# Transposing the first tile of y with a DMA and reordering VectorE's last stage-one work

## What is computed

```python
def fake_quant(x, scale, zp):
    q = clip(round(x / scale + zp), 0, 255)
    return (q - zp) * scale

def lora_ffn(x, W_up, gate_w, expert_bias, lora_A, lora_B):
    logits = x @ gate_w.T + expert_bias            # 4 experts
    one_hot = jax.nn.one_hot(argmax(logits), 4)
    base = x @ W_up.T
    z = einsum('nh,erh->ner', x, lora_A)           # rank 8
    delta = einsum('neh,ne->nh', einsum('ner,ehr->neh', z, lora_B), one_hot)
    return base + delta

x = x + tanh(g_xattn) * (fake_quant(layernorm(x)) @ fake_quant(ctx))
x = x + tanh(g_ffn) * lora_ffn(layernorm(x))
```

## Time and profile before

| | us |
|---|---|
| median of 3 runs | 956.85 (956.59 to 957.64) |
| the profiled execution, its own time | 955.6 |
| span of the profile | 953.8 |
| TensorE busy in matmuls | 933.3 |
| VectorE busy | 472.6 |
| ScalarE busy | 231.3 |
| GpSimd busy | 16.6 |

### The profile page before, as it was taken

How to read it: one execution, slowest core, us unless ns; L and a number is a source line. 1 busy time by engine, 2 the same in 40 slices (tenths; PEclk the granted TensorE clock), 3 DMA queues, 4 the chain that set the end, 5 groups by cost and what they waited for, 6 DMA issues and landing times.

```text
span 953.8 us, 12333 instructions
## 1 busy us (share of the span) xinstructions
PE 933.3 (98%) x5190; PEld 498.3 (52%) x5214; DVE 472.6 (50%) x1022; ACT 231.3 (24%) x192; POOL 16.6 (2%) x40
## 2 busy tenths in 40 slices
PE   4999999999999999999999999999999999999998
PEld 2444444444555555555555555555555555555554
DVE  7774757787775725244351625344342615343322
ACT  6976777776540100000000000000000000000000
POOL 0000100000000000000000000000000000000000
PEclk9999999999999999999999999999999999999999
DMA  8999977679564422222223222222223222121211
GB/s 347 421 416 415 397 291 276 223 299 316 222 181 133 133 89 45 89 45 89 56 78 95 75 96 45 89 45 89 45 89 89 68 66 45 45 45 45 45 45 45
DMA packets 85370, 137.37 MB, mean 144 GB/s; under 512 B 70224, under 2 KB 70368, under 8 KB 71008
## 3 DMA queue, kind: packets, MB, share of 16 engines
q1 hardware_dynamic: 79376, 94.83, 31.2%
q0 software_dynamic: 3488, 24.92, 6.7%
q10 hardware_dynamic: 2448, 16.78, 4.3%
HBM read 90.38 MB, written 29.37 MB: 126 GB/s over the span
## 4 chain that ended last, share of the span: by engine, by line
PE 96%; ACT 2%; DVE 1%; DMA 1%; issue 0%; SPq 0%; ACTq 0%; DVEq 0%
PE bank L1131 71%; PE bank L1049 22%; PE bank L1140 1%; PE bank L1026 1%; DMA rows<-in_x 1%; ACT arena L446 1%; ACT halves L416 0%; ACT rows_T L434 0%; DVE bn L638 0%; PE bank L1123 0%; DVE arena L709 0%; SPq L294 0%; PE bank L1146 0%; DVE rows L826 0%; DVE ln L642 0%
## 5 line engine op out<-in xcount | busy, mean ns | idle before, releaser
L1131 PE MATMUL bank<-arena,rows_T 128*128 128x416 f16 (+1 forms) x3840 | 683.0, 339 | 0.0
L1131 PEld LDWEIGHTS bank<-arena,rows_T 128*128 128x128 f16 x3840 | 372.5, 97 | 304.5
L1049 PE MATMUL bank<-arena,rows_T 128*128 128x512 bf16 x1000 | 222.0, 380 | 2.7 <-DVE arena L709 1.5
L1049 PEld LDWEIGHTS bank<-arena,rows_T 128*128 128x128 bf16 x1024 | 99.5, 98 | 119.8 <-issue 2.9
L826 DVE SCALAR_TENSOR_TENSOR rows<-bank,derived,rows 128x416 f32<-128x416 f32 (+2 forms) x80 | 49.7, 640 | 210.6 <-PE bank L1131 210.6
L485 ACT ACTIVATE z_stack_T<-bank 96x128 f16<-96x128 f16 x16 | 4.4, 273 | 555.3 <-PE bank L1146 555.3
L638 DVE BATCH_NORM_STATS2 bn<-rows 128x6 f32<-128x512 f32 x124 | 76.7, 678 | 4.2 <-DMA rows<-in_x 3.7
L766 DVE SCALAR_TENSOR_TENSOR route<-bank,derived,scal 128x4 f32<-128x4 f32 x16 | 3.5, 221 | 110.2 <-PE bank L1131 110.2
L699 DVE SCALAR_TENSOR_TENSOR rows<-bank,derived,rows 128x512 f32<-128x512 f32 x60 | 44.8, 747 | 25.7 <-PE bank L1049 25.2
L834 DVE SCALAR_TENSOR_TENSOR rows<-bank,z_back_scale,rows 128x512 f32<-128x512 f32 x64 | 45.1, 746 | 9.6 <-PE bank L1140 5.6
L739 DVE SCALAR_TENSOR_TENSOR halves<-normed,ln,halves 128x2048 f16<-128x2048 f32 x14 | 32.9, 2351 | 29.0 <-ACT halves L479 29.0
(11 more groups left out here) (107 smaller groups left out, 287.8 us busy)
## 6 DMA issues: line engine op xcount, KB each, us to landing
arena<-in_ctx SPq DMA_DIRECT2D x22, 1024.0 KB, 16.8
stage<-in_w SPq DMA_DIRECT2D x17, 1042.0 KB, 6.2
out<-rows ACTq DMA_DIRECT2D x15, 1024.0 KB, 3.9
h_scratch<-rows POOLq DMA_DIRECT2D x11, 1024.0 KB, 8.7
rows<-h_scratch SPq DMA_DIRECT2D x11, 1024.0 KB, 4.8
stage<-in_ctx SPq DMA_DIRECT2D x10, 1024.0 KB, 9.1
rows<-in_x POOLq DMA_DIRECT2D x10, 1024.0 KB, 9.0
normed<-in_w SPq DMA_DIRECT2D x7, 1042.0 KB, 6.8
```

The source lines that it names most:

```text
L1049: mm = mmul(bk, q1T[:, t % 4, kt, :], Q(b, n, kt), start=(kt == 0), stop=(kt == KT - 1 and not slow), skip_group_check=True)
L1131: mm = mmul(bank[c][:, 0:b - a], YT[:, s % 2, yh, kt, :], W(kt, wh, a, b), start=(first and kt == kts[0] and yh == 0 and wh == 0), stop=(k ...
```

## The change

Tile 0 of y is transposed by DMA as well. SyncE issues `y_transpose(0)` between W's loads 15 and 16, and the 32 TensorE transposes are gone. `yT_out` becomes `yT_scale`, which scales `YT` in place in SBUF for both tiles and, for tile 0, waits for the DMA transpose. On VectorE `epi(15, 1)` and `epi(15, 2)` now stand ahead of `w_low(8)`, and the second to fourth scalings of tile 0 come later, between and behind `w_low(9)` to `w_low(11)`. The counts of the semaphore `s_dt` go up by one transfer wherever it is waited for.

```diff
@@ -35,7 +35,6 @@
     LEAD = 3
     KEEP = 4
 
-    BY_PE = 1
     UNSCALED = 2
     HALF = KT // 2
 
@@ -170,8 +169,6 @@
 
         bank = [es.enter_context(nc.psum_tensor(f"bank{i}", [P, NB], F32)) for i in range(8)]
         TR = [bank[5][:, :], bank[6][:, :]]
-
-        YB = [TR[0], TR[1], bank[7][:, :], TR[0]]
         ZP = bank[7][:, :].bitcast(F16)[0:ZR, 0:P]
 
         s_scal = sem("scal_loaded"); s_braw = sem("b_loaded"); s_bs = sem("b_abs_sum"); s_bp = sem("b_pow")
@@ -195,7 +192,7 @@
         s_sum = sem("w_abs_sum"); s_wp = sem("w_pow"); s_wa = sem("w_scale"); s_hi = sem("w_high")
         s_lo = sem("w_ready")
         s_pm = sem("pow_max"); s_PM = sem("pow_max_all")
-        s_yh = sem("y_high"); s_yl = sem("y_low"); s_yt = sem("yT_group"); s_ye = sem("yT_out")
+        s_yh = sem("y_high"); s_yl = sem("y_low"); s_ye = sem("yT_scaled")
         s_wc = sem("w_back_scale"); s_wr0 = sem("w_back_row_parked"); s_wr = sem("w_back_row_loaded")
         s_xt = {t: sem(f"q1_transposed_by_dma{t}") for t in BY_DMA}; s_dt = sem("y_transposed_by_dma")
         s_m2 = sem("chunk2_done"); s_dl = sem("delta_done"); s_rt = sem("route_step"); s_zs = sem("z_stack_ready"); s_gl = sem("z_back_scale_ready")
@@ -312,6 +309,15 @@
             row(5)
             for c in range(16, CT):
                 ctx_tile(c)
+            def y_transpose(s):
+                sp.wait_ge(s_yl, s + 1)
+                if s < UNSCALED:
+                    sp.wait_ge(s_mm, place[(13 if s == 0 else 15, NCH - 1)] + 1)
+                else:
+                    sp.wait_ge(s_m2, 5 * (s - 1))
+                sp.dma_start_transpose(YT[:, s % 2].rearrange("p h k m -> p (h k) m"),
+                                       HL[:, :, :].rearrange("p h d -> p (h d)")).then_inc(s_dt, 16)
+
             def q1_transpose(t):
                 sp.wait_ge(s_q1, t + 1)
                 sp.wait_ge(s_mm, place[(t - 4, NCH - 1)] + 1)
@@ -323,24 +329,18 @@
             for i in range(12, 14):
                 load_w(i)
             q1_transpose(15)
-            for i in range(14, KT + 8):
+            for i in range(14, KT):
                 load_w(i)
-
-            def y_transpose(s):
-                sp.wait_ge(s_yl, s + 1)
-                if s == 1:
-                    sp.wait_ge(s_mm, place[(TILES - 1, NCH - 1)] + 1)
-                else:
-                    sp.wait_ge(s_m2, 5 * (s - 1))
-                sp.dma_start_transpose(YT[:, s % 2].rearrange("p h k m -> p (h k) m"),
-                                       HL[:, :, :].rearrange("p h d -> p (h d)")).then_inc(s_dt, 16)
+            y_transpose(0)
+            for i in range(KT, KT + 8):
+                load_w(i)
 
             sp.wait_ge(s_wc, 1)
             sp.dma_start(wrow_d.rearrange("k p -> p k"), wc[:, :],
                          allow_slow_non_contiguous=True).then_inc(s_wr0, 16)
             sp.wait_ge(s_wr0, 16)
             y_transpose(1)
-            sp.wait_ge(s_dt, 16)
+            sp.wait_ge(s_dt, 32)
             sp.dma_start(WR, wrow_d.rearrange("k p -> (k p)").unsqueeze(0).to_broadcast([P, D])).then_inc(s_wr, 16)
             for s in range(UNSCALED, TILES):
                 if s + 3 < TILES:
@@ -398,7 +398,7 @@
             nc.gpsimd.dma_start(br[:, :], brow_d.rearrange("k o -> (k o)").unsqueeze(0).to_broadcast(
                 [P, E * R])).then_inc(s_br, 16)
             pool.wait_ge(s_bst, 1)
-            pool.wait_ge(s_dt, 16)
+            pool.wait_ge(s_dt, 32)
             row(TILES + KEEP)
 
         @block.scalar
@@ -467,11 +467,8 @@
                 act.wait_ge(s_norm, s + 1)
                 if s == 0:
                     transposed(act, TILES - 1)
-                elif s <= BY_PE:
-                    act.wait_ge(s_yt, 4 * s)
-                    act.wait_ge(s_yl, s)
                 else:
-                    act.wait_ge(s_dt, 16 * (s - BY_PE))
+                    act.wait_ge(s_dt, 16 * s)
                 u = TILES + s
                 if s < UNSCALED:
                     A(HL[:, 0, :], Xt(u), ACT.Identity, bias=L(u, "nmr"), scale=L(u, "rstd")).then_inc(s_yh, 1)
@@ -732,24 +729,16 @@
             def y_low(s):
                 dve.wait_ge(s_yh, s + 1)
                 if s < UNSCALED:
-                    if s >= 1:
-                        dve.wait_ge(s_yt, 4 * s)
                     v.tensor_tensor(HL[:, 1, :], T[:, 0:D], HL[:, 0, :], ALU.subtract).then_inc(s_yl, 1)
                 else:
                     v.scalar_tensor_tensor(out=HL[:, 1, :], in0=T[:, 0:D], scalar=L(TILES + s, "rstd"), in1=HL[:, 0, :],
                                            op0=ALU.mult, op1=ALU.subtract).then_inc(s_yl, 1)
 
-            def yT_out(s, g):
-                dst = YT[:, s % 2, :, 4 * g:4 * g + 4, :]
-                if s < BY_PE:
-                    dve.wait_ge(s_yt, 4 * s + g + 1)
-                    dve.wait_ge(s_mm, place[(13, NCH - 1)] + 1)
-                    src = YB[g].bitcast(F16).rearrange("p (h a m) -> p h a m", h=2, a=4)
-                else:
-                    dve.wait_ge(s_dt, 16)
-                    src = dst
+            def yT_scale(s, g):
+                dve.wait_ge(s_dt, 16 * (s + 1))
+                part = YT[:, s % 2, :, 4 * g:4 * g + 4, :]
                 back = wc[:, 4 * g:4 * g + 4].unsqueeze(1).unsqueeze(3).to_broadcast([P, 2, 4, P])
-                v.tensor_tensor(dst, src, back, ALU.mult).then_inc(s_ye, 1)
+                v.tensor_tensor(part, part, back, ALU.mult).then_inc(s_ye, 1)
 
             def route(s):
                 base = LINKS * s
@@ -946,17 +935,17 @@
             dve.sem_inc(s_wc, 1)
             step(v.tensor_scalar(V["sc2"], V["PM"], UN, None, ALU.mult))
             step(v.tensor_tensor(V["gs"], V["sc2"], V["tf"], ALU.mult))
-            yT_out(0, 0)
+            yT_scale(0, 0)
+            epi(15, 1)
+            epi(15, 2)
             w_low(8)
-            epi(15, 1)
-            yT_out(0, 1)
-            epi(15, 2)
-            yT_out(0, 2)
             epi(15, 3)
             w_low(9)
+            yT_scale(0, 1)
             w_low(10)
             w_low(11)
-            yT_out(0, 3)
+            yT_scale(0, 2)
+            yT_scale(0, 3)
             b_scale()
             w_low(12)
             w_low(13)
@@ -966,12 +955,12 @@
             y_low(1)
             b_low()
             route(0)
-            yT_out(1, 0)
-            yT_out(1, 1)
+            yT_scale(1, 0)
+            yT_scale(1, 1)
             for c in range(3):
                 epi2(0, c)
-            yT_out(1, 2)
-            yT_out(1, 3)
+            yT_scale(1, 2)
+            yT_scale(1, 3)
             epi2(0, 3)
             epi2(0, 4)
 
@@ -1102,27 +1091,6 @@
                         chunk(t, n, slow)
                         if n == 0 and t + 1 in BY_TENSOR:
                             transposes(t + 1)
-                        if n == 1 and t == TILES - 1:
-                            y_transposes(0, 0)
-                            y_transposes(0, 1)
-                            y_transposes(0, 2)
-                        if n == 2 and t == TILES - 1:
-                            y_transposes(0, 3)
-
-            def y_transposes(s, g):
-                if g == 0:
-                    pe.wait_ge(s_yl, s + 1)
-                if s == 0 and g < 2:
-                    half_out(TILES - 1, g)
-                elif s == 0 and g == 2:
-                    pe.wait_ge(s_epi, NCH * (TILES - 1))
-                else:
-                    pe.wait_ge(s_ye, 1)
-                for i in range(8):
-                    h, k = i // 4, 4 * g + i % 4
-                    mm = nc.tensor.transpose(YB[g].bitcast(F16)[:, i * P:(i + 1) * P],
-                                             HL[:, h, k * P:(k + 1) * P], idh[:, :])
-                mm.then_inc(s_yt, 1)
 
             def products(s, c, kts, first):
                 a, b = CUT[c], CUT[c + 1]
@@ -1150,7 +1118,7 @@
 
             def tile2(s):
                 if s >= UNSCALED:
-                    pe.wait_ge(s_dt, 16 * (s - BY_PE + 1))
+                    pe.wait_ge(s_dt, 16 * (s + 1))
                 for c in range(3):
                     free2(s, c)
                     if s == 1 and c < 2:
```

## The result

Over 22 runs each, the changed kernel takes 954.67 us (953.77 to 956.94) and the kernel before 956.54 us (955.68 to 958.14). The medians differ by 1.87 us. The ratio, which uses all the runs, is 0.9983, with a 95% interval of 0.9976 to 0.9989: 1.6 us less, between 1.1 and 2.3. The forecast was 1.4 us. The change is clear of zero, but under the 0.2% (1.9 us) that the prediction set as what can be told from no change.

A forecast was written before the change was run, and what follows sets the result against it. The prediction took TensorE, busy 98% of the span, as the bound: 1.79 us of removed transposes less a 0.4 us wait at tile 1 gives 1.4, so 956.85 - 1.4 = 955.5 us, range 954.8 to 957.5.

The forecast's parts named there:

- The removed work: TensorE, end of stage one: 32 transposes at 0.056 us apiece leave the path, 1.79 us, the most that can be won.
- The transpose in the queue: SyncE's queue: tile 0's transpose issued at 240.2, SyncE released at 246 (bounds 245.0 to 247.4), load 16 landing at 251.5.
- The sign on the first scaling: VectorE and ScalarE: first scaling after 251.1, or ScalarE idle for load 16 beyond 252, would refute the queue step.
- the step on the queue: SyncE: the transpose lands by 248.5, before the first scaling at 251.08, and load 16 lands between 249.7 and 253.6.
- No stall at epi(15,3): Start of stage two: VectorE's last stage-one epilogue ends at 257.66, TensorE asks at 258.23; no stall, by 0.6 us.
- w_low(15): Last five blocks of tile 0, stage two: done at 284.5, wanted by TensorE at 285.8; margin 1.3 us.
- w_low(12) 0.5 us sooner: VectorE in stage two: w_low(12) starts at 268.6 against 269.08, so load 23 and the row-scale store come 0.5 us sooner.
- The wait of 0.4 us at tile 1: Start of tile 1, stage two: TensorE waits 0.4 us for epi2(0,0), which follows tile 1's DMA transpose and two scalings.
- rival 1: Whole 1.79 us arrives if tile 1's transpose is 0.5 us or more early: 955.1 us; chance 0.17.
- Rival 2: W's loads come late, 0.5 us stall at epi(15,3), net gain 0.5: 956.3, or 957.3 with further delay; chance 0.21.
- rival 3: Slower: transpose blocks the queue longer, delaying load 16, w_high(8), w_low(8), epi(15,3); 959.2 if load 16 lands at 256.6; chance 0.10.

The follow-up runs named there:

- experiment 2: Changed kernel with the 32 transposes of y's first tile also issued on TensorE, results unread; ratio 1.0000 against the kernel before.
- experiment 1: Kernel before with only VectorE's new order, tile 0 of y still transposed on TensorE; ratio 1.0004 against the kernel before.
- experiment 5: Changed kernel with VectorE's old order, w_low(8) first and scalings between the epilogues; ratio 1.0012 against the kernel before.
- experiment 6: Changed kernel with tile 0's DMA transpose issued after W's loads 16 and 17 instead of ahead of them; ratio 1.0010 against the kernel before.
- experiment 7: Changed kernel with tile 0 transposed by DMA a second time after the first landed, ahead of load 16; ratio 1.0060 against the kernel before.
- experiment 4: Changed kernel with the wait for the row-scale store's landing moved behind the issue of tile 1's transpose; ratio 0.9980 against the kernel before.
- experiment 3: Changed kernel without tile 0's DMA transpose, its product made from stale data; ratio 0.9983 against the kernel before.
- experiment 9: Changed kernel with stage one's tile 14 DMA transpose issued ahead of W's loads 10 and 11; ratio 0.9989 against the kernel before.
- experiment 8: Changed kernel with stage one's tile 13 also transposed by DMA, behind load 8, instead of 16 TensorE transposes; ratio 0.9993 against the kernel before.
- experiment 10: Changed kernel with tile 13 transposed by DMA and tile 14's transpose ahead of loads 10 and 11; ratio 1.0010 against the kernel before.
- experiment 11: Experiment 10's kernel with VectorE's epi(15,3) ahead of w_low(8) and w_low(12) ahead of tile 0's last two scalings; ratio 1.0002 against the kernel before.
- experiment 12: Experiment 11's kernel with tile 15's DMA transpose issued ahead of load 13 instead of behind it; ratio 0.9996 against the kernel before.

## Why the prediction was right, point by point

- **The removed work** was sized exactly: 1.79 us between the marks, the same again put back by experiment 2, and nothing from the order (experiment 1).
- **The transpose in the queue.** Forecast: SyncE held until 246 for a stage two at 256.64, so load 16 out 10.6 us ahead of it. Measured 258.91 - 248.47 = 10.4. Load 16 landed 5.8 us after its issue (5.5 taken). Both bounds held, but the close match is two misses that cancel: the transpose went out at 243.63, 15.3 us ahead of stage two where 16.4 was forecast (y_high(0) ran later), and held SyncE 4.8 us where 5.8 was taken: load 15, which landed at 246.0, did not slow it.
- **The sign on the first scaling** did show. The prediction named a first scaling later than 251.1, or ScalarE idle for load 16 beyond 252, as refuting the step on the queue. Taken from the first mark, the first scaling came 1.1 us later than before (254.45 - 206.21 = 48.24 against 251.08 - 203.95 = 47.13), and ScalarE waited for load 16 until 254.37, which is 252.1 on the clock of before. The delay arose ahead of the new transpose: stage one's transpose of tile 15 held SyncE 7.69 us where it had held 6.59, so load 15 and abs_sum(15), from which the scale is made, came 1.1 us later. The new transpose had landed at 250.3, 4 us before VectorE wanted it. So the sign was badly chosen rather than the step wrong.
- **No stall at epi(15,3)**: forecast with 0.6 us to spare, measured 260.5 - 259.9 = 0.6. Experiments 5, 6 and 7 show that this is a thin margin: each takes it away and TensorE pays 2.1, 2.5 and 4.6 us. w_low(15) was done 1.4 us before it was wanted (284.28 + 2.3 = 286.6 against 258.91 + 165 x 0.1765 = 288.0); 1.3 was forecast.
- **w_low(12) 0.5 us sooner** was wrong by 0.9 in the profiled execution. It started 12.9 us after the start of stage two; forecast 268.6 - 256.6 = 12.0. The step that failed held VectorE alone to decide: w_low(11) waited 0.92 us for ScalarE, whose load 19 is released only by w_low(8) and landed 5.1 us after its issue at 259.32. In the trace of experiment 4, which differs only in a later wait, w_low(11) waited 0.16 and w_low(12) came 269.58 - 257.47 = 12.1 behind, as forecast. So this hangs on how late an execution gets load 16. It cost nothing.
- **The wait of 0.4 us at tile 1** did not come; it was the one term mis-sized. In this trace there are 301.3 - 299.6 = 1.7 us to spare. Two durations were taken from a single row: the store of the scales, 16.5 us, and the landing of tile 1's transpose, 8.25. They are 15.4 and 6.7 now. The earlier trace rows had 6.7 as the median of 15 transposes and would have been the better choice. So the traces show rival 1, the whole 1.79; the measured 1.6, with its interval of 1.1 to 2.3, cannot tell it from the forecast 1.4. That 1.4 lies so near is therefore no evidence for the wait: the medians' 1.87 lies nearer to rival 1, and neither the runs nor experiment 4 can settle whether unprofiled executions ever wait there.
- **Rival 2** did not happen and **rival 3** had its mechanism right: it is experiment 7. Its price was too low, since it left out the clock.

Why the transpose of tile 1 landed after 8.2 us in the kernel before and after 6.7 in the changed one can be read, in the main, from the single DMA transfers that the traces record. In the three kernels where it took 8.2 (before, experiments 1 and 2, the ones with the 32 transposes on TensorE), one 16 KB transfer of queue q8, which the page calls "instruction", began 5.9 to 6.1 us after the issue, and the transpose's last transfers ended at 7.4 to 7.5 us. In the changed kernel and experiments 3, 4, 5, 6 and 9 no transfer of that queue ran beside it, the last ones ended at 6.2 us, and it landed after 6.7. (In experiment 7 it took 6.8 and in 8 and 10 to 12 between 7.2 and 7.9, with transfers of q8 or of q14, also "instruction", in the first 2.4 us of it.) So the 8.25 us that the prediction built its wait on came from a transpose with such a transfer beside it. What stays open is whether the fetch causes the delay, since no run moves it alone, and whether removing 32 instructions is what moved it away.

## What to carry to other kernels

When TensorE is 98% busy, price a removed instruction by the distance between starts, not by its duration (0.056 us against 0.22 here), and expect exactly that sum if the replacement stays off the path. Before moving work to a DMA queue, follow what is queued behind it to the engine that waits in order: here load, high half, low half, epilogue. The new order on VectorE, worth nothing by itself, is what kept that chain from stalling TensorE. A stall should be priced above its own length where it can lower the clock, and a time to landing should be the median of its kind, picked by how many loads stand ahead in the queue, not the one row at hand.

## What the runs showed of the hardware

- **A DMA transpose is slow by what stands ahead of it.** The same 128x4096 transpose held SyncE 4.8 us and landed after 6.7 behind one load that had almost landed, and took 7.45 and 9.7 behind two. The half-size one for tile 14 landed after 11.3 us behind two loads (10.4 to 12.9 over the traces) and after 5.1 to 6.9 ahead of them (experiments 9 to 12).
- **Slow DMA transposes also go with a fetch of instructions.** In the 14 traces, 151 of y's transposes shared their time with no transfer of another queue and with no load, and all landed 6.65 to 6.84 us after their issue. Of the 57 that overlapped only with transfers of the queues q8 and q14, both "instruction" on the page, 25 took over 7 us. Seven took 8.2 to 8.3, each with one 16 KB transfer of q8 that began 5.8 to 6.1 us in, and seven took 9.2, each with one of both queues there. These go together in the records; no run separates cause and effect.
- **A pause of TensorE can cost more than its length.** After 4.46 us idle the granted clock fell to 0.57 for 4 us (1.2 GHz for most of it instead of 2.4) and 1.7 us more were lost. It also fell after the pauses of 2.22 us in experiment 8 (39.77 us for the 216 matmuls) and 2.96 us in experiment 10 (39.54), but not after one of 2.26 us in experiment 6 (38.08). TensorE had been busy without a break for tens of us ahead of all four. What decides between them these runs don't show. TensorE's slices behind the pause, experiment 8:

```profile
262.00:264.00 2.00, 2.00 (x7) 0.50 0.86 342
264.00:266.00 2.00, 2.00 (x10) 0.67 0.95 333
```

- **The start of the kernel scatters by 2 us.** The changed kernel's profiled execution waited 3.36 us for the first quantized tile, where the one of before waited 1.46, and its clock stood at 0.57 between 24 and 28 us. TensorE's first transposes, before and after:

```profile
14.59 1.86 PE L1026 MATMUL bank<-ident_bf,halves 128*128 128x128 bf16 x16 [1.46 <-DVE halves L692]
```

```profile
16.85 1.86 PE L1015 MATMUL bank<-ident_bf,halves 128*128 128x128 bf16 x16 [3.36 <-DVE halves L689]
```

  At the first mark it was 2.26 us behind. Over the ten traces that have this mark, it lies between 203.91 and 206.21 us. This is larger than the effect under study, and it is why spans of single executions could not show it while the marks could.
